# Cross-attention on one core: the probabilities are turned by two DMA transposes per batch instead of on TensorE, and a batch's output product follows the next batch's scores

## The reference

```
q = layernorm(x) @ Wq;  k = ctx @ Wk;  v = ctx @ Wv          (per batch)
x = x + concat_heads(softmax(q k^T / sqrt(32)) v) @ Wo + bo
x = x + attention over all the tokens of a batch (one head, causal, one softmax over the matrix)
x = x + feed-forward with binarised weights (512 -> 2048 -> 512, gelu)
```

## Time and profile before

| | |
|---|---|
| runs | 2922.21, 2919.47, 2920.38 us; median 2920.38 |
| profiled execution: span, first to last instruction | 2917.1 us (the page has no other time for it; the median of the runs is 3.3 us above it) |
| TensorE busy | 2794.1 us, 96% of the span |
| VectorE busy | 1668.3 us, 57% |
| ScalarE busy | 1267.4 us, 43% |
| GpSimd busy | 776.4 us, 27% |
| DMA | 118.49 MB, mean 41 GB/s |
| mean granted TensorE clock | 0.980 |

### The profile page before, as it was taken

The page is one execution under the profiler, slowest core; times in us unless marked ns, Lnnn a source line. Parts: engine busy times, 40 slices in busy tenths (PEclk is TensorE's granted clock), DMA queues, the critical chain, the costliest instruction groups (busy, mean ns, idle before and its releaser), DMA issues. The chain is left out here.

```text
span 2917.1 us, 54809 instructions
## 1 busy us (share of the span) xinstructions
PE 2794.1 (96%) x18492; PEld 1704.0 (58%) x18492; DVE 1668.3 (57%) x3620; ACT 1267.4 (43%) x2954; POOL 776.4 (27%) x1530
## 2 busy tenths in 40 slices
PE   7999999999999999999999999957999999899999
PEld 4455555555555555555555555534666666566666
DVE  7555555555555555555555555556665666656664
ACT  4344444444444444444444444423433443344444
POOL 2233333333333333333333333211111111111110
PEclk9999999999999999999999999978999999999999
DMA  4211111111111111111111111022000000000000
GB/s 143 83 56 55 62 41 40 40 48 41 40 40 48 41 40 40 48 41 40 40 48 41 40 40 48 13 84 66 15 30 15 15 14 22 22 14 14 14 23 15
DMA packets 65959, 118.49 MB, mean 41 GB/s; under 512 B 12016, under 2 KB 32496, under 8 KB 65392
## 3 DMA queue, kind: packets, MB, share of 16 engines
q1 hardware_dynamic: 65904, 117.76, 12.4%
HBM read 109.06 MB, written 8.65 MB: 40 GB/s over the span
## 5 line engine op out<-in xcount | busy, mean ns | idle before, releaser
L656 DVE SCALAR_TENSOR_TENSOR kT_lo<-psum,kT_hi 128x512 f16<-128x512 f32 x256 | 177.1, 692 | 440.2 <-ACT kT_hi L587 440.2
L591 ACT ACTIVATE v_hi<-psum 128x512 f16<-128x512 f32 x256 | 152.8, 597 | 552.7 <-PE psum L746 552.7
L746 PE MATMUL psum<-c_hi,xWk_hi 128*128 128x512 f16 x1024 | 388.1, 379 | 2.3 <-PEq L136 2.3
L746 PE MATMUL psum<-xWv_hi,c_hi 128*128 128x512 f16 x1024 | 388.3, 379 | 0.0
L746 PE MATMUL psum<-xWv_lo,c_hi 128*128 128x512 f16 x1024 | 388.1, 379 | 0.0
L746 PE MATMUL psum<-xWv_hi,c_lo 128*128 128x512 f16 x1024 | 388.1, 379 | 0.0
L746 PE MATMUL psum<-c_lo,xWk_hi 128*128 128x512 f16 x1024 | 388.1, 379 | 0.0
L746 PE MATMUL psum<-c_hi,xWk_lo 128*128 128x512 f16 x1024 | 388.1, 379 | 0.0
L118 POOL TENSOR_TENSOR c_lo<-ctx_raw,c_hi 128x1024 f16<-128x1024 f32 x128 | 272.5, 2129 | 429.8 <-ACT c_hi L583 419.2
L662 DVE SCALAR_TENSOR_TENSOR v_lo<-psum,v_hi 128x512 f16<-128x512 f32 x256 | 177.1, 692 | 360.4 <-ACT v_hi L591 360.4
L597 ACT ACTIVATE e<-psum,neg_max 128x257 f32<-128x257 f32 x512 | 236.3, 474 | 281.9 <-DVE neg_max L651 281.9
(11 more groups left out here) (195 smaller groups left out, 5986.9 us busy)
## 6 DMA issues: line engine op xcount, KB each, us to landing
ctx_raw<-in_ctx_main SPq DMA_DIRECT2D x128, 512.0 KB, 3.3
xs<-in_x SPq DMA_DIRECT2D x8, 1024.0 KB, 5.5
v_rep<-v_last_rows SPq DMA_DIRECT2D x512, 16.0 KB, 2.3
xb<-in_x SPq DMA_DIRECT2D x16, 512.0 KB, 3.3
out<-res_out SPq DMA_DIRECT2D x32, 256.0 KB, 2.0
ffn_raw<-in_w_t SPq DMA_DIRECT2D x11, 512.0 KB, 3.4
late_raw<-in_late_w SPq DMA_DIRECT2D x4, 1024.0 KB, 4.7
res<-in_w_t SPq DMA_DIRECT2D x5, 512.0 KB, 3.5
```

The source lines that it names most:

```text
L591: nc.scalar.mul(v_hi[u][:, t, :], v_bank(t), W_UNSCALE).then_inc(v_hi_done, 1)
L656: nc.vector.scalar_tensor_tensor(out=kT_lo[r][:, m, :, 0:S], in0=k_bank(m), scalar=W_UNSCALE, in1=kT_hi[r][:, m, :, 0:S], op0=ALU.mult, op ...
L746: mm = nc.tensor.matmul(bank, a, b, start=(n == 0), stop=(n == len(steps) - 1))
```

## The change

TensorE's transposes are gone, and with them their PSUM banks. ScalarE casts the 1024 exponentials of a row directly to fp16 high halves in SBUF (`p_hi`), in one instruction, VectorE subtracts for `p_lo` in one, and SyncE turns both with a DMA transpose each, SBUF to SBUF, into `pT_hi` and `pT_lo`. SyncE waits for `p_lo` before both, and issues two of the four `v_rep` loads ahead of them and the other two and the context load behind them.

The order changes with it. On TensorE a step is now keys, keys, values(b+1, 0), values(b+1, 1), score(b+1), outputs(b). Scores of b + 1 wait for the exponentials of b alone. The output product goes to bank 5, which it shares with every second key chunk: the odd key chunk waits for the gather of the last output, and the output product for the low half of the odd key chunk. ScalarE computes the exponentials of b + 1, then the output's high half of b, then the high probabilities of b + 1; VectorE the maxima of b + 1, then gather, normalisation and low half of b's output, then the low probabilities of b + 1.

```diff
@@ -445,8 +445,10 @@
-        pT_hi = sb_in(ctx, "pT_hi", [P, ST, D], F16)
-        pT_lo = sb_in(ctx, "pT_lo", [P, ST, D], F16)
+        p_hi = sb_in(ctx, "p_hi", [P, KC * S], F16)
+        p_lo = sb_in(ctx, "p_lo", [P, KC * S], F16)
+        pT_hi = sb_in(ctx, "pT_hi", [P, KC * ST, P], F16)
+        pT_lo = sb_in(ctx, "pT_lo", [P, KC * ST, P], F16)
...
@@ -478,7 +480,7 @@
-        out_bank = psum[:, 3, :].rearrange("p (g n) -> p g n", g=KC)
+        out_bank = psum[:, 5, :].rearrange("p (g n) -> p g n", g=KC)
...
@@ -488,9 +490,9 @@
-            def load_last(b, u):
+            def load_last(b, u, heads=range(HPG)):
                 past(sp, last_done, b - 1)
-                for h in range(HPG):
+                for h in heads:
...
+            def step(b, u, context=True, last=True):
+
+                sp.wait_ge(p_lo_done, b + 1)
+                past(sp, pv_ps, b)
+                if last:
+                    load_last(b + 2, u, range(2))
+                sp.dma_start_transpose(pT_hi[:, :, :], p_hi[:, :]).then_inc(pT_hi_landed, 16)
+                sp.dma_start_transpose(pT_lo[:, :, :], p_lo[:, :]).then_inc(pT_lo_landed, 16)
+                if last:
+                    load_last(b + 2, u, range(2, HPG))
+                if context:
+                    load_context(nc, sp, ctx_main, contexts, b + 6, u)
 
             def quad(i, late=False, end=False):
                 if late:
                     load_late(i)
                 for u in range(4):
                     b = i * 4 + u
-                    if not end or b + 6 < BATCH:
-                        load_context(nc, sp, ctx_main, contexts, b + 6, u)
-                    if not end or b + 2 < BATCH:
-                        load_last(b + 2, u)
+                    step(b, u, context=not end or b + 6 < BATCH, last=not end or b + 2 < BATCH)
...
@@ -593,14 +605,17 @@
             def exponentials(b):
                 act.wait_ge(neg_done, b + 1)
                 past(act, last_done, b)
+                past(act, p_lo_done, b)
+                past(act, inv_done, b)
                 for g in range(KC):
...
             def high_probs(b):
-                for t in range(ST):
-                    act.wait_ge(p_ps, ST * b + t + 1)
-                    nc.scalar.copy(pT_hi[:, t, :], psum[:, t, :]).then_inc(pT_hi_done, 1)
+
+                past(act, pT_hi_landed, 16 * b)
+                act.wait_ge(e_done, KC * (b + 1))
+                nc.scalar.copy(p_hi.rearrange("p (g s) -> p g s", g=KC), e[:, :, 0:S]).then_inc(p_hi_done, 1)
...
@@ -613,25 +628,25 @@
 
             def step(i, u, more=True, keys=True, ahead=True):
                 b = i * 4 + u
-                exponentials(b)
                 if keys:
                     for m in (2 * (u % 2), 2 * (u % 2) + 1):
                         high_keys(i * 2 + u // 2 + 1, 1 - u // 2, m)
-                elif more:
-                    high_values(b + 1, (u + 1) % 2, 0)
-                high_probs(b)
                 if ahead:
                     high_context(b + 4, u, (i + 1) * 2 + u // 2 + 1)
-                if keys:
-                    high_values(b + 1, (u + 1) % 2, 0)
                 if more:
-                    high_values(b + 1, (u + 1) % 2, 1)
+                    for t in range(ST):
+                        high_values(b + 1, (u + 1) % 2, t)
+                    exponentials(b + 1)
                 high_output(b)
+                if more:
+                    high_probs(b + 1)
 
             for m in range(KC):
                 high_keys(0, 0, m)
             for t in range(ST):
                 high_values(0, 0, t)
+            exponentials(0)
+            high_probs(0)
             with act.Fori(0, LATE) as i:
...
             def low_probs(b):
-                for t in range(ST):
-                    dve.wait_ge(pT_hi_done, ST * b + t + 1)
-                    nc.vector.tensor_tensor(pT_lo[:, t, :], psum[:, t, :], pT_hi[:, t, :],
-                                            ALU.subtract).then_inc(pT_lo_done, 1)
+
+                dve.wait_ge(p_hi_done, b + 1)
+                past(dve, pT_lo_landed, 16 * b)
+                nc.vector.tensor_tensor(p_lo.rearrange("p (g s) -> p g s", g=KC), e[:, :, 0:S],
+                                        p_hi.rearrange("p (g s) -> p g s", g=KC),
+                                        ALU.subtract).then_inc(p_lo_done, 1)
...
@@ -709,26 +726,24 @@
 
             def step(i, u, more=True, keys=True):
                 b = i * 4 + u
-                maxima(b)
+                low_probs(b)
+                inverse(b)
                 if keys:
                     for m in (2 * (u % 2), 2 * (u % 2) + 1):
                         low_keys(i * 2 + u // 2 + 1, 1 - u // 2, m)
-                elif more:
-                    low_values(b + 1, (u + 1) % 2, 0)
-                low_probs(b)
-                inverse(b)
-                if keys:
-                    low_values(b + 1, (u + 1) % 2, 0)
+                if more:
+                    for t in range(ST):
+                        low_values(b + 1, (u + 1) % 2, t)
+                    maxima(b + 1)
                 gather_output(b)
                 finish_output(b)
-                if more:
-                    low_values(b + 1, (u + 1) % 2, 1)
                 low_output(b)
 
             for m in range(KC):
                 low_keys(0, 0, m)
             for t in range(ST):
                 low_values(0, 0, t)
+            maxima(0)
             with dve.Fori(0, LATE) as i:
...
@@ -760,55 +775,50 @@
-            def score(i, u):
-                b = i * 4 + u
+            def score(b, u, pairs):
+
                 pe.wait_ge(bd_ready, 2 * HPG * (b + 1))
-                pe.wait_ge(k_col, 2 * (i * 2 + u // 2 + 1))
-                pe.wait_ge(k_lo_done, KC * (i * 2 + u // 2 + 1))
-                past(pe, pT_lo_done, ST * b)
-                past(pe, o_sum_done, HPG * b)
+                pe.wait_ge(k_col, 2 * pairs)
+                pe.wait_ge(k_lo_done, KC * pairs)
+                past(pe, e_done, KC * b)
                 for g in range(KC):
                     mm = run(psum[:, g, 0:S + 1],
                              [(q[:, g, :, :].rearrange("p h l -> p (h l)"), k[u // 2][:, g, u % 2, 0:S + 1])
                               for q, k in passes(bd_hi, bd_lo, kT_hi, kT_lo)])
                 mm.then_inc(s_ps, 1)
 
-            def probs(b):
-                pe.wait_ge(e_done, KC * (b + 1))
-                for t in range(ST):
-                    for g in range(KC):
-                        mm = nc.tensor.transpose(psum[:, t, g * P:(g + 1) * P], e[:, g, t * P:(t + 1) * P],
-                                                 ident[:, :])
-                    mm.then_inc(p_ps, 1)
-
-            def outputs(b, u):
-                pe.wait_ge(pT_lo_done, ST * (b + 1))
+            def outputs(b, u, keys_done):
+                pe.wait_ge(pT_hi_landed, 16 * (b + 1))
+                pe.wait_ge(pT_lo_landed, 16 * (b + 1))
                 pe.wait_ge(v_lo_done, ST * (b + 1))
+                pe.wait_ge(k_lo_done, keys_done)
                 for g in range(KC):
                     cols = slice(g * P, (g + 1) * P)
-                    mm = run(out_bank[:, g, :], [(p[:, t, cols], v[:, t, cols]) for t in range(ST)
+                    mm = run(out_bank[:, g, :], [(p[:, g * ST + t, :], v[:, t, cols]) for t in range(ST)
...
             def step(i, u, more=True, key=True):
                 b = i * 4 + u
-                score(i, u)
+                pair = i * 2 + u // 2 + 1
                 if key:
-                    for m in (2 * (u % 2), 2 * (u % 2) + 1):
-                        keys(i * 2 + u // 2 + 1, 1 - u // 2, m)
-                elif more:
-                    values(b + 1, (u + 1) % 4, 0)
-                probs(b)
-                if key:
-                    values(b + 1, (u + 1) % 4, 0)
-                outputs(b, u)
+                    m = 2 * (u % 2)
+                    keys(pair, 1 - u // 2, m)
+                    past(pe, o_sum_done, HPG * b)
+                    keys(pair, 1 - u // 2, m + 1)
+                else:
+                    pe.wait_ge(o_sum_done, HPG * b)
                 if more:
-                    values(b + 1, (u + 1) % 4, 1)
+                    for t in range(ST):
+                        values(b + 1, (u + 1) % 4, t)
+                    score(b + 1, (u + 1) % 4, i * 2 + (u + 1) // 2 + 1)
+                outputs(b, u, KC * pair + m + 2 if key else KC * BATCH // 2)
 
             for m in range(KC):
                 keys(0, 0, m)
             values(0, 0, 0)
             values(0, 0, 1)
+            score(0, 0, 1)
```

More of the change, by code:

```diff
@@ L464, in cross_attention @@
         names = ["bd_clear", "bd_ready", "k_col", "last_done", "k_ps", "v_ps",
-                 "s_ps", "p_ps", "pv_ps", "k_hi_done", "k_lo_done", "v_hi_done", "v_lo_done", "max_done",
-                 "neg_done", "e_done", "pT_hi_done", "pT_lo_done", "inv_done", "o_sum_done",
```

(8 more changed lines are left out.)

## The result

The changed kernel takes 2815.16 us (median of 4 runs, 2814.66 to 2815.95), the kernel before in the same comparison 2919.93 us (2919.16 to 2922.21): a ratio of 0.964, 95% interval 0.9626 to 0.9654. The forecast was 2814, the range 2804 to 2895. The span fell from 2917.1 to 2812.6 us.

A forecast was written before the change was run, and what follows sets the result against it. TensorE's never-resting stream was taken as the bound: 126 x 0.87 = 109.6 us less, and +3, takes the 2917.1 span to 2810.5; with 3.3 us of median above span, about 2814. Range 2804 to 2895.

The forecast's parts named there:

- The bound and the term of the sum: TensorE's stream sets the stage's cost; removing eight transposes saves 0.87 us, taking a batch from 13.90 to 13.03 us.
- The chain: From scores' end through maxima, exponentials and casts to the DMA turns: first turn out at 7.35 us, output product at 13.03.
- table of steps: Times laid out from the score stream's end: maxima start at 0.31 us, the gather at 1.80, low halves end at 6.35.
- The unknown price: The two DMA turns, absent from the trace: taken as 0.45 + 3.3 = 3.75 us, landing 1.9 us early.
- 5.68 us of cover: Time per batch from issue of the first DMA turn, 7.35, to TensorE reaching the output product, 13.03.
- First 16 batches: Late weights' splitting shifts the work before the turns about 1.35 us, leaving 0.6 of margin; +3 us, bounds 0 and 20.
- The end: Last two batches, with no keys to hide behind: 23.0 us before, 22.9 after, so no gain or cost; bounds -1 and +5.
- The sum: Whole kernel: 126 x 0.87 = 109.6 less, and +3, takes the span from 2917.1 to 2810.5 us, about 2814 measured.
- In series: Rival: the two DMA turns run one after the other, 2836 to 2917 us, middle about 2850; chance 0.25.
- Slower: Rival: DMA turns take longer than the time available to hide them, e.g. 3451 us, far end 6760; chance 0.14.
- point of decision: For DMA turns making the kernel slower: both together need over 6.85 us, since 7.05 + 6.85 = 13.90 a batch.
- Doesn't do what it says: Rival: TensorE meets another wait, the gather's or the landing, and gives the 0.87 us back, 2920 us; chance 0.03.

The follow-up runs named there:

- E1: The changed kernel's new order, but TensorE still turns the probabilities with eight fp32 transposes and there are no DMA transposes: 2919.86 us, ratio 1.0.
- E5: The changed kernel with one more DMA transpose of the high halves per batch, into a spare tile, ahead of the two: 2887.69 us, ratio 0.9884.
- E3: The changed kernel without the two DMA transposes; the output product reads the probabilities unturned, so it computes another attention output: 2804.57 us.
- E6: The changed kernel with two more DMA transposes of the high halves per batch, ahead of the two: 3085.80 us, ratio 1.0567.
- E7: The changed kernel with each half turned in eight DMA transposes of one 128x128 block instead of one of 128x1024: 5020.93 us, ratio 1.719.
- E2: The changed kernel with DMA transposes, but the output product ahead of the next scores again, ScalarE and VectorE following that order: 3325.75 us, ratio 1.14.
- E8: The changed kernel with three more DMA transposes per batch ahead of the two: 3351.69 us, ratio 1.1475.

## Why the prediction was right

- **The bound and the term of the sum.** TensorE's stream was the stage's cost and the transposes' 0.87 us a batch its only change. E1 shows it from the other side: the same order with the transposes takes 13.90 us a batch and 2919.86 in all. Predicted 13.03 a batch, measured 13.02. "Provided TensorE still never waits" held from 400 to 1700 us.
- **The chain.** The first turn was to go out at 7.35 us after the scores' end. In the batch whose outputs start at 1006.49 (t = 0) the next one's goes out at 1013.71, so at 7.22. The maxima start 0.11 earlier than in the table of steps, and the low subtraction, priced at 1.28 by the pair, takes 1.22.
- **The unknown price** came out right as a conclusion and wrong as a term. "I take 0.45 + 3.3 = 3.75": the hold was 1.29 and not the 0.45 of a plain issue, and the landing 3.1 to 3.2, so 4.4. With the restart of TensorE behind the landing the margin was 1.03 us (E5), not 1.9. The forecast survived because both lie inside the 5.68 us of cover. The prediction's estimate of 1.0 us of data per turn, from the 261 GB/s of the Trainium skill, "DMA: Bandwidth & Descriptors", section "Latency and other measured facts", is borne out as a slope only: a turn of 256 KB lands 0.8 us later than a block of 32 KB, 224 KB more (229,376 bytes, 287 GB/s), and one of 512 KB 1.1 us later than one of 256 KB (238 GB/s), with landings that the view rounds to 0.1 us. Most of a turn's time doesn't go with its size: a block of 32 KB takes 2.4 us to land.
- **First 16 batches.** +3 us was forecast, and 5.4 us came, of which the waits name 3.2. The prediction had 0.6 us of margin left in the ordinary ones and gave the whole price to the three at the late loads. But with the real margin of 1.03 and the chain 1.35 later none was left, and each of the 16 started its outputs late; the 25 us of E5 show the same.
- **The end.** "These two batches gain nothing and cost nothing": they cost 1.1 us. One part left out is the wait of the step without keys for the gather, 1.4 us, where TensorE has no keys to do meanwhile; the odd key product itself never waited.
- **The sum** (106.6 less, against 104.5 in the span) came out close in part by luck, since its errors go both ways: the last two points are too low a cost by 3.7 us together, and a gain of 1.9 is missing. The prediction measured the end from the scores of batch 126 in both kernels. The outputs of batch 125 stood ahead of that mark before and stand behind it now, so up to the mark the changed kernel gains another 1.3 us, which the sum lacks. E3, whose TensorE never waits there, shows it: from the maxima of batch 0 to those of 126 it is 1750.67 - 1639.18 = 111.5 us shorter than the kernel before, which is 126 x 0.87 = 109.6 and the 1.3, with 0.6 for the rounding of 0.87. So the parts are 111.5 - 5.6 (first batches, by the same maxima) - 1.1 (end) = 104.8 against 104.5 measured in the span.
- **The rivals.** *In series*: in the sense of the second turn's landing, no; it lands 3.1 us after its own issue. But the queue's hold puts them 1.29 apart, which is the part of that rival that was true. *Slower*: its point of decision was 6.85 us from first turn to landing. Counted from the first extra turn, E5 has 5.8 us (1007.39 to 1010.03 + 3.2) and is 33 us faster than the kernel before; E6 has some 7.2 and is 165 slower. The crossing lies between, as it should. By the 1309 ns a block of the Trainium skill, "VectorE: DVE Perf Modes", section "The three transpose paths", the prediction estimated 4720 for sixteen blocks one after another. That is near what a block costs as an instruction of its own (1.25 us of hold in E7, 5021 us in all); eight blocks in one instruction cost the same hold. *Doesn't do what it says*: out.
- **What my expectations missed afterwards** is one thing three times: a wait that recurs in each batch costs more than its length. In E2 the clock and VectorE's order added to it, in E6 the loop was as long as with the maxima ahead (7.3 us and not 7.05 from output to first turn), in E8 the clock cost 1.3 us, but not in every batch.

What stays open is why the clock fell behind some waits and not behind others of the same length (3.01 and 2.97 us in E8).

## What to carry to other kernels

Where TensorE never rests, anything taken out of its stream is time, by the distance of starts and not by the busy time; and a slower path is free as long as the whole chain, queue holds included, ends before TensorE comes back. Move the consumer first and only then the work: with the outputs ahead of the next scores the DMA turns cost 406 us (E2, part of it by VectorE's order there) instead of saving 105. And issue a DMA transpose over as many columns as there are, because each instruction holds its queue.

## What the runs showed of the hardware

- A DMA transpose on SyncE's queue holds it 1.25 us for 128x128, 1.24 to 1.31 for 128x1024, 1.92 for 128x2048 (16-bit, SBUF to SBUF), and lands after 2.4, 3.1 to 3.2 and 4.3 us (medians). A plain copy holds it 0.35 to 0.45.
- The turns of the changed kernel are 270,337 packets more than before (336,296 against 65,959), 1056 for each turn of 256 KB, so 256 bytes a packet with some over; the context load beside them lands in 3.3 us as before, v_rep in 1.7 where it was 2.3, a late 1 MB load in 5.1 where it was 4.7.
- Between 400 and 1700 us TensorE's granted clock stayed 1.00 with a wait of 1.7 us in each batch (E6) and was 0.92 with 2.5 (E2) and 2.8 (E8), with stretches at the lower of its two levels (1.2 and 2.4 GHz) behind the waits: 24 output products took 2.52 us against 1.33, in 58 of 76 batches in E2, 54 of 76 in E8 and one of 87 in E6.
